# Two evictions on ScalarE, one of them with its product on TensorE, moved from odd to even iterations of a software-pipelined attention

## What is computed

```python
latents = _layernorm(x)
xn = layer_norm(ctx, g1, b1)
ln_lat = layer_norm(latents, g2, b2)
q = ln_lat @ Wq
kv = jnp.concatenate([xn, ln_lat], axis=1) @ Wkv          # 1024 keys
k, v = jnp.split(kv, 2, axis=-1)
weight = jnp.einsum('bhld,bhnd->bhln', q * scale, k * scale)
weight = jnp.where(full_mask[:, None, None, :], weight, neg)
weight = jax.nn.softmax(weight, axis=-1)
out = jnp.einsum('bhln,bhnd->bhld', weight, v)
x = x + jnp.tanh(g_xattn[3]) * (out @ Wout)
```

## Time and profile before

| | us |
|---|---|
| median of 3 runs | 3132.04 |
| lowest, highest | 3129.66, 3149.77 |
| the profiled execution | 3149.77 |
| its span | 3148.0 |
| mean granted clock of TensorE | 0.887 of full |

### The profile page before, as it was taken

How to read it: one execution, slowest core, us unless ns; L and a number is a source line. 1 busy time by engine, 2 the same in 40 slices (tenths; PEclk the granted TensorE clock), 3 DMA queues, 4 the chain that set the end, 5 groups by cost and what they waited for, 6 DMA issues and landing times. The chain is left out here.

```text
span 3148.0 us, 35249 instructions
## 1 busy us (share of the span) xinstructions
PE 2544.1 (81%) x12416; PEld 1351.4 (43%) x12416; DVE 1815.8 (58%) x4079; ACT 1171.6 (37%) x2079; POOL 789.4 (25%) x494
## 2 busy tenths in 40 slices
PE   6885865175587869969989978989987998987996
PEld 2332323032355534535554444545453545453554
DVE  5664743113787747247748437766726774825774
ACT  1432331021232415236535215643414653513662
POOL 1004123443000004014414204332302432401441
PEclk8987975587587869989999989999998999998998
DMA  7310005285420020034431024431012442002442
GB/s 234 110 29 15 15 14 149 80 295 181 151 88 7 8 95 1 1 101 118 106 90 43 7 82 101 113 98 65 7 68 75 117 105 94 1 14 88 114 120 68
DMA packets 113982, 257.04 MB, mean 82 GB/s; under 512 B 37223, under 2 KB 57319, under 8 KB 107787
## 3 DMA queue, kind: packets, MB, share of 16 engines
q1 hardware_dynamic: 93210, 218.68, 22.9%
q10 hardware_dynamic: 13424, 27.55, 3.5%
q0 software_dynamic: 7168, 8.50, 0.9%
HBM read 119.81 MB, written 29.74 MB: 48 GB/s over the span
## 5 line engine op out<-in xcount | busy, mean ns | idle before, releaser
L862 POOL TENSOR_SCALAR pbuf<-pbuf,recip 128x1024 f32<-128x1024 f32 x128 | 364.7, 2849 | 991.9 <-DVE recip L766 991.9
L811 ACT ACTIVATE pbuf<-ps,least 128x1024 f32<-128x1024 f32 x256 | 284.4, 1113 | 301.9 <-DVE least L759 213.5
L759 DVE CUSTOM_DVE_ANT_0 ps<-ps,mask 128x1024 f32<-128x1024 f32 x256 | 307.9, 1244 | 137.7 <-PE ps L690 136.4
L587 POOL TENSOR_SCALAR pbuf<-pbuf,recip 128x512 f32<-128x512 f32 x128 | 200.4, 1577 | 479.0 <-DVE recip L508 479.0
L690 PE MATMUL ps<-kH,qT 64*128 64x512 f32 x1024 | 272.3, 653 | 52.4 <-ACT pbuf L811 49.2
L715 PE MATMUL ps<-work,vh 128*64 128x256 f32 x2048 | 252.1, 390 | 2.3 <-ACT wide L831 2.3
L558 ACT ACTIVATE pbuf<-ps,least 128x512 f32<-128x512 f32 x256 | 172.7, 686 | 161.0 <-DVE least L498 160.9
L773 DVE STREAM_TRANSPOSE pbuf<-pbuf 128x2048 f32<-128x2048 f32 (+1 forms) x128 | 226.3, 1768 | 0.0
L1507 ACT ACTIVATE early<-ps 128x1536 f32<-128x1536 f32 x86 | 124.0, 1441 | 271.4 <-PE ps L1340 207.6
L1580 DVE TENSOR_REDUCE mh<-ps 128x3 f32<-128x1536 f32 x86 | 150.0, 1745 | 105.4 <-PE ps L1329 65.3
L996 POOL DMA_INDIRECT slot_token<-info,place x128 | 126.9, 992 | 242.7 <-DVE info L1745 189.9
(11 more groups left out here) (346 smaller groups left out, 4125.4 us busy)
## 6 DMA issues: line engine op xcount, KB each, us to landing
work<-pbuf SPq DMA_DIRECT2D x768, 96.0 KB, 2.6
work<-pbuf ACTq DMA_DIRECT2D x256, 96.0 KB, 3.0
early<-in_L_wgu SPq DMA_DIRECT2D x24, 768.0 KB
expert_rows<-zero_rows SPq DMA_DIRECT2D x16, 1024.0 KB, 11.6
yg<-expert_rows SPq DMA_DIRECT2D x16, 1024.0 KB, 6.2
early<-in_L_wd SPq DMA_DIRECT2D x24, 384.0 KB
arena<-in_L_wo SPq DMA_DIRECT2D x8, 1024.0 KB, 10.1
arena<-in_L_wff SPq DMA_DIRECT2D x4, 2048.0 KB, 9.4
```

Source lines behind the costliest of these rows:

```text
L587: nc.gpsimd.tensor_scalar(x, x, recip[:, n % 8:n % 8 + 1], None, mult).then_inc(probs_ready[1], 1)
L759: nc.vector.tensor_tensor_reduce(out=x, in0=x, in1=mask, scale=1.0, scalar=FMAX, op0=add, op1=ALU.min, accum_out=least[:, n % 8:n % 8 + 1])\
L811: nc.scalar.activation(to, x, ACT.Exp, bias=least[:, n % 8:n % 8 + 1], scale=-1.0, accum_out=sums[:, n % 8:n % 8 + 1]).then_inc(taken, 1)
L862: nc.gpsimd.tensor_scalar(unit(n), unit(n), recip[:, n % 8:n % 8 + 1], None, mult).then_inc(pool_divided, 1)
```

## The change

Two edits. In `scalar`, `keep_values(h)` leaves iteration 2h+5, where it stood between the division and the moves, for iteration 2h+6, where it stands behind both exponentials and `keep_turned` and ahead of the jobs' evictions; the one that has no such iteration follows behind the loop. In `jobs3`, the first value job of a group goes from slot 3 to slot 1, that is from the end of iteration 4g+1 to iteration 4g.

```diff
--- before.py
+++ after.py
@@ -839,6 +839,8 @@
                 exponent(2 * p + 3)
             if p >= 2 and p % 2 == 0:
                 keep_turned(p // 2 - 1)
+            if p >= 6 and p % 2 == 0:
+                keep_values(p // 2 - 3)
             for n in (2 * p, 2 * p + 1):
                 for job in before[n]:
                     if job[0] is not None and keeper(job) == "a":
@@ -847,11 +849,10 @@
                         done[0] += 1
             if p + 1 < N:
                 divide(2 * p + 3)
-            if p >= 5 and p % 2:
-                keep_values((p - 5) // 2)
             if p % 2:
                 move(act, p // 2, True)
         keep_turned(N // 2 - 1)
+        keep_values(N // 2 - 3)
         keep_values(N // 2 - 2)
         keep_values(N // 2 - 1)
 
@@ -2880,7 +2881,7 @@
                 return (lambda pe: value_product(g, kb, 7),
                         lambda act: nc.scalar.activation(vh[g % 2][:, 4 * kb:4 * kb + 4, :], by_token(7), ACT.Copy), "a")
 
-            mine = [(3, "", vals(g, 0)), (6, "values", vals(g, 1))] if g else []
+            mine = [(1, "", vals(g, 0)), (6, "values", vals(g, 1))] if g else []
             following = [(0, "", q_job(wqx, latT, g + 1)), (2, "", keys(g + 1, 0)), (4, "scores", keys(g + 1, 1))] if g + 1 < HP else []
             return following + mine
```

## The result

| | before | after |
|---|---|---|
| median, us | 3135.75 (4 runs) | 3261.21 (4 runs) |
| lowest, highest | 3129.66, 3149.77 | 3254.19, 3269.49 |
| ratio, 95% interval | | 1.0395 (1.0351 to 1.0440) |
| span of the profiled execution | 3148.0 | 3263.3 |

What follows compares the result with a forecast made beforehand. No engine was taken as the bound, but a ring through PE, VectorE, ScalarE and DMA moves. Groups add 84 us, last groups and tails 2, clock falls 27: 3132+113 = 3245 us, range 3190 to 3300.

Steps and rivals of the forecast that it cites:

- The even iteration 4g: First iteration of a four-iteration group: value product waits for the query copy; next E at E+9.32, leg 12.12 us from 9.16.
- E: Start of an iteration's first exponential on ScalarE; E+9.32 means 9.32 us after it.
- the leg: Time from an odd iteration's transposition end (T), over the next even iteration, to the following odd iteration's E.
- keep_values in 4g+2: Group's third iteration: `values` waits for `keep_values` until E+3.52, nothing hides it; next E at E+8.82, leg 11.62 us.
- The gain in 4g+1: Group's second iteration: scores no longer stand behind the value product, so 0.93 us a group is gained.
- The rival that it pays: Even iterations have room for what they are given; each group keeps 0.93 us, 22 us faster, 3110 us; chance 0.07.
- That only `keep_values` costs: Rival: the value product in 4g could go at once; 74 us slower, 3206 us; chance 0.14.
- That nothing changes: Rival: waits for transfers shrink by what is added, sum near 0, 3132 us; chance 0.07.
- PE's clock: PE dry 2.8 us in 4g+2; clock falls to half in two groups of three, 16 times 1.7, 27 us.
- The rival with a fall in every even iteration: PE's clock falls twice a group: 48 x 1.7 = 82 us in place of 27, 3300 us; chance 0.14.
- The rest: Last group of each batch and the tails: +2 us for all four batches, range -10 to +14.
- the old stall: In 4g+2 of the kernel before, VectorE waits 2.40 us for PE's scores, queued behind value product and key copy.

Runs made afterwards that it cites:

- e5: Kernel before with the value job in slot 1, and the first half of `values` put ahead of that slot's jobs on PE: ratio 0.9965.
- e1: Kernel before with only the value job moved to slot 1, `keep_values` left in its old place: 3196.85 us against 3123.34, ratio 1.0230.
- e3: Changed kernel with `keep_values` first in the even iteration, ahead of both exponentials: 3199.74 us, ratio 1.0238 to the kernel before.
- e8: e1 with the transpositions of `turn_last` done three times over in iterations 4g: 3164.16 us against 3124.07 for the kernel before, ratio 1.0126.
- e10: Changed kernel with `turn_last`'s transpositions done three times over in iterations 4g+2: 3236.75 us against 3263.18 for the changed kernel; ratio 1.0359 to the kernel before.
- e2: Kernel before with only `keep_values` moved, the value job left in slot 3: 3272.84 us against 3123.34, ratio 1.0482.

## Why the prediction was right

*The even iteration 4g.* The step had the next E at E+9.32; without a fall it is E+9.25 in the profile, and the leg 12.04 for 12.12. e5 shows the cause to be the place in PE's queue: with the job behind `values` the leg is 10.48.

*keep_values in 4g+2.* Forecast E+8.82 and 11.62 for the leg; measured E+8.85 and 11.64 where the clock stayed. PE waits 3.01 us there, ended by `wide<-ps`. e1 and e3 take the wait away by two routes and bring the leg to 9.65 and 9.80.

*The gain in 4g+1.* Forecast 0.93 a group, with ScalarE's issue of moves next. E of 4g+2 comes at T+2.79 in the profile. The rival that it pays is refuted by the point it named: scores were needed by E+2.63 and came at E+5.91. That only `keep_values` costs is refuted by e1, where the value job alone costs 2.3%, and by e8, where it still costs 1.3% with most falls gone. That nothing changes, since waits for transfers shrink by what is added, is out by the ratio: these waits fell by 63 us, and the group grew all the same.

*PE's clock.* 27 us for 16 falls were forecast. In the leg over 4g+2 there are 13; the 11 legs without one average 11.72 us and the 13 with one 13.58, which makes 24 us, and e10 bears that out. Fewer legs were hit than assumed, and each cost more (1.9 us for 1.7; three of the 13 are 14.6 us long). That the product of the two comes out is partly luck, as two groups in three was a guess. Three falls in leg 4g (13.66 us in the profile for 12.04) add 5 us. The rival with a fall in every even iteration is out: leg 4g stayed at 12.0 to 12.3 in 21 of 24. None of the 17 holes of 1.35 to 1.71 us ahead of the value product in 4g was followed by a fall, and all three of 2.5 us were; but the same idle 2.90 us of the windows above are followed by one once and not the next time. So the Trainium skill's rule that long holes put the clock back (TensorE: Matmul & The Clock Gate, Why this matters for your kernels) is borne out in its direction and not as a certainty.

*The rest.* +2 us was counted for last groups and tails. In the two profiles they are 3.1 and 4.1 us longer, 7 us in all: the term was too small, inside the -10 to +14 kept for it. The whole comes out at 3261.21 us for 3245, 16 more. Of these, 3.7 are the base, as the kernel before came out at 3135.75 in four runs and not at the 3132.04 the forecast stood on; 5 are the last groups and tails; about 5 are the groups (116 us for 84+27). The others lie within what one execution differs from the next. Of the 4.8 us that a group grew by, the two waits without falls make up 3.5 and the falls about 1.2.

What the prediction didn't see is how the two moves relate. Alone they cost 2.30% and 4.82%, together 3.95%. In e2 the new wait of 4g+2 meets the old stall there, and the one of 4g draws a fall each time. In e1 the value job's hole is 2.3 us and more in most groups and draws falls that the changed kernel, which has PE busy until later there (a hole of 1.35 to 1.71), mostly does not have.

One thing wasn't tried: `values(h)` waits for `keep_values(h-1)` though it writes the other half of bank 6, so a wait for `keep_values(h-2)` would do for the data. With the looser wait, ScalarE would read one half of the bank while PE writes the other, with nothing to order them. The Trainium skill (PSUM — Partial Sum Buffer, PSUM bank collisions raise a hardware error) says that two engines in one bank and quadrant collide whichever columns they touch; no run here shows it.

## What to carry to other kernels

Before a small eviction is moved to where its engine looks idle, look for who waits on its semaphore: the price is set by what stands ahead of it in its own queue at that moment, here two exponentials and a copy. A product that must wait for an eviction belongs behind the work that needs no wait, since everything behind it in the in-order queue waits with it; the same job cost 2.3% ahead of `values` and gained 0.35% behind it. And an eviction that stands behind a wait for another engine may be free a step earlier: that one swap on VectorE is worth 0.9% here.

## What I had not expected of the hardware

The clock's falls don't go by the length of the hole alone. In the changed kernel the holes of 3.01 us ahead of `values` in 4g+2 were followed by a slowed leg in 13 of 24 groups; in e1 the holes ahead of the value product, 2.33 us in the rows above, were followed by one in 17 of 24, with legs of 13.56 us and more; and in e2 holes of 2.29 us ahead of `values` in 4g+2 were followed by one in only 2 of 24. What decides between them stays open. Cheap work into a hole is a remedy, if one must keep the hole: 16 redundant transpositions in a group gave back 19 us in the groups and 22 to 26 us of the changed kernel's time.
